# Moving the split of the output weights to the end of VectorE's step, and holding GpSimd's running sums 2 to 7 until the last low part of the step is written

## The chip, the cores and the metric

The kernel runs on one core of a Trainium2 chip. The metric is the device time of one execution in microseconds (us). The engines are TensorE (PE in the profile, with its weight loads as PEld), VectorE (DVE), ScalarE (ACT), GpSimd (POOL) and SyncE (SP), which starts the transfers.

## What is computed

Causal attention with 16 heads over two sequences of 1024 tokens, a layernorm, a mixture-of-experts block, and a second layernorm. The part that the change touches is the attention:

```python
q = rmsnorm(q, q_norm_w);  k = rmsnorm(k, k_norm_w)
q = apply_rope(q, ...);    k = apply_rope(k, ...)
scores = jnp.einsum('bhtd,bhsd->bhts', q, k) * scale
scores = LOGIT_SOFTCAP * jnp.tanh(scores / LOGIT_SOFTCAP)
scores = jnp.where(mask, -jnp.inf, scores)
attn = jax.nn.softmax(scores, axis=-1)
out = jnp.einsum('bhts,bhsd->bhtd', attn, v)      # B=2, H=16, T=1024, d=128
return out @ wo.T
```

## The kernel before

**Precision.** Every large product is made of three: each operand is kept as a high part (a rounded copy, suffix `_hi`) and a low part (what the rounding left, `_lo`), and TensorE adds hi·hi, hi·lo and lo·hi (`mm3`, lines 417 to 419). For most operands ScalarE writes the high part and VectorE the low one (`lo_of`, line 1098: source minus high part). For weights VectorE writes both (`split`, lines 1108 and 1098).

**Steps.** Attention is 32 steps, one per head and sequence. Heads go in pairs: the four steps of a pair have `q` = 0 to 3, where `k = q % 2` is the head of the pair and `q // 2` the sequence. I call them q0, q1, q2 and q3; there are 8 pairs. Step `s` computes the eight score tiles of its head and sequence (tile `j` is 128 keys by the `T - 128 j` queries from them on: 1024, 896, 768, 640, 512, 384, 256 and 128 columns). Within the same step TensorE also projects the queries and keys of step `s + 1` and finishes step `s - 1`: its last value products, the sums of its probabilities and its output projection. The code calls the work on step `s - 1` `old` and that on step `s + 1` `new`; the last step of all has no `new`.

**One tile's way.** TensorE `scores` to PSUM; ScalarE tanh and exp into `praw` in SBUF; GpSimd `mask` on the diagonal 128 columns (line 959); ScalarE the high part `prob_hi`; VectorE the low part `prob_lo` (`tile`, line 1202; signals `plo_done`); TensorE `values`. Besides, GpSimd adds the eight tiles of a step up in `pacc` (`accumulate`, lines 972 and 976: a copy for tile 0, then seven additions, from 896 down to 128 columns, which I call running sums 1 to 7). Each addition waits for the one ahead of it. When all eight are in, TensorE's `sums` multiplies `pacc` with ones (line 451), and VectorE turns that into `rsum`, by which it scales the output projection.

**Queues.** Each engine runs its own instructions in the order in which the code lists them, step after step; nothing but semaphores couples the engines. In a step TensorE's order is: projections `q0`, `q1` of the next step, old `values` 3, `scores` 0 (which waits for `qlo_done`, the low part of the step's queries), in odd steps a projection of values `vc`, `k0`, old `values` 4, `k1`, `scores` 1, old `values` 5 to 7, `ss` (sums of squares), `scores` 2 and 3, old `sums`, then the output projections `op0` to `op3` among further scores and values. Projections take turns in two PSUM banks: each waits until the second one ahead of it has been read (`pj_free`). The first two, `q0` and `q1`, are read by VectorE's copies to `qraw` (line 1165).

VectorE's order is in `step` below. Its last three pieces are the low part of the values `vb` or `vd`, the scaling of the next step's queries `scale_raw` (line 1183), and their split `split_queries` (`qhat_hi`, `qhat_lo`). The scaling needs a row of factors that GpSimd computes (`rq`, line 943, behind masks 0 and 1), VectorE transposes (line 1179), and SyncE sends through DRAM to all partitions (`rqB`).

The split of the output weights `wo` of one head (`split_output_weights`, two instructions on 128 by 256) runs in q0 and q1. Its product is read by TensorE at `op0` of the step after.

Of the kernel before, what the change touches and what calls it, by code (L numbers as in the profile page):

```python
# [27 lines left out]
TT = T // P  # L28
# [21 lines left out]
RING = TT  # L50
# [85 lines left out]
def block_kernel(nc, x, xT_d, wqkv_d, wo_d, qn, kn, cos_d, sin_d, gw_d, wgu_d, wd_d, wsgu_d, wsd_d, out):  # L136
# [5 lines left out]
    with ctx:  # L142
# [3 lines left out]
        def sem(name):  # L146
            return ctx.enter_context(nc.semaphore(name))
# [132 lines left out]
        mask_done, phi_done, plo_done = sem("mask_done"), sem("phi_done"), sem("plo_done")  # L280
# [646 lines left out]
        def _(pool):  # L927
# [12 lines left out]
            def rms_queries(b, count):  # L940

                pool.wait_ge(pj_free, count)
                nc.gpsimd.tensor_tensor(rq[:, 0:TT], var[:, b, 0:TT], mhalf[:, 0:TT], ALU.pow).then_inc(rq_done, 1)

            def rms_keys(b):
                nc.gpsimd.tensor_tensor(rk[:, b, :], var[:, b, TT:2 * TT], mhalf[:, TT:2 * TT], ALU.pow).then_inc(rk_done, 1)
# [6 lines left out]
            def mask(s, b, j):  # L953

                t = s * TT + j
                pool.wait_ge(exp_done, t + 1)
                diag = praw[:, raw_at(b, j)][:, 0:P]
                pool.sem_inc(waited, 1)
                nc.gpsimd.affine_select(out=diag, in_=diag, compare_op=ALU.is_ge, fill=0.0, base=0,  # L959
                                        pattern=[[1, P]], channel_multiplier=-1).then_inc(mask_done, 1)  # L960

            def accumulate(s, b, j):

                t = s * TT + j
                if j == 0 and not (isinstance(s, int) and s == 0):
                    pool.wait_ge(rsum_done, s)
                pool.wait_ge(mask_done, t + 1)
                raw = praw[:, raw_at(b, j)]
                if j == 0:

                    pool.sem_inc(waited, 1)
                    nc.gpsimd.tensor_copy(pacc[:, 0:P], raw[:, 0:P]).then_inc(pacc_done, 1)
                else:
                    before = praw[:, raw_at(b, 0)][:, P:T] if j == 1 else pacc[:, P * j:T]
                    pool.wait_ge(pacc_done, t + RING)
                    nc.gpsimd.tensor_tensor(pacc[:, P * j:T], before, raw, ALU.add).then_inc(pacc_done, 1)  # L976

            def next_head_weights(p, s):
                pool.wait_ge(qf_done, s + 1)
                pool.sem_inc(waited, 1)  # L980
                nc.gpsimd.tensor_copy(gcur[:, :], ghead[:, bass.ds(p * 2 + 2, 2)]).then_inc(gcur_done, 1)

            def step(st):

                s, k, old, new = st.s, st.k, st.old, st.new
                if old:
                    mask(s - 1, 1 - k, 6)
                    mask(s - 1, 1 - k, 7)
                    for j in range(TT):
                        accumulate(s - 1, 1 - k, j)  # L990
                if new and st.q == 3:
                    next_head_weights(st.pair, s)
                mask(s, k, 0)
                mask(s, k, 1)
                if new:
                    rms_queries(1 - k, st.unit("ss")[0])
                mask(s, k, 2)
                mask(s, k, 3)
                if new:
                    rms_keys(1 - k)  # L1000
                mask(s, k, 4)
                mask(s, k, 5)

            pool.wait_ge(zeros_out, 16 * ((2 * ACCR // P * D + T - 1) // T + 1))
            for q in range(STEPS):
                step(Step(0, q, "first"))
# [3 lines left out]
            for q in range(STEPS):  # L1010
                step(Step(NP_ - 1, q, "last"))
# [78 lines left out]
        def _(dve):  # L1090
# [5 lines left out]
            def lo_of(dst, x_, hi, done):  # L1096

                v.tensor_tensor(dst, x_, hi.bitcast(F32), ALU.subtract).then_inc(done, 1)  # L1098
# [7 lines left out]
            def split(pair_, at_, src, hi_sem, n, lo_sem):  # L1106

                v.tensor_copy(pair_[0][at_], src).then_inc(hi_sem, 1)
                dve.wait_ge(hi_sem, n)
                lo_of(pair_[1][at_], src, pair_[0][at_], lo_sem)  # L1110

            def split_next_weights(p, e, count):

                dve.wait_ge(w_in[e], p * 16 + 16)
                if count is not None:
                    dve.wait_ge(pj_done, count)
                split(wqk, (ALL, e), wraw[:, e], whi_done, p * 2 + e + 1, wlo_done)
# [52 lines left out]
            def values_in(what, group, count, bank_no):  # L1170
                dve.wait_ge(pj_done, count)
                dve.wait_ge(vhi_done, group + 1)
                two = slice(2 * V_TILES[what], 2 * V_TILES[what] + 2)
                lo_of(vS[1][:, two].rearrange("p j e d -> p (j e d)"), ps[:, bank_no, :],
                      vS[0][:, two].rearrange("p j e d -> p (j e d)"), pj_free)

            def turn_rms(step):
                dve.wait_ge(rq_done, step + 1)
                v.transpose(rqT[:, :], rq[:, :]).then_inc(rqT_done, 1)
# [19 lines left out]
            def tile(s, b, j):  # L1199
                dve.wait_ge(phi_done, s * TT + j + 1)  # L1200
                n = T - P * j
                lo_of(prob[1][:, AT[j]:AT[j] + n], praw[:, raw_at(b, j)], prob[0][:, AT[j]:AT[j] + n], plo_done)
# [11 lines left out]
            def output_lo(s):  # L1214
                dve.wait_ge(ohi_done, s + 1)
                lo_of(oT[1][:, :], ps[:, 4:6, :].rearrange("p k n -> p (k n)"), oT[0][:, :], o_evac)
# [8 lines left out]
            def split_output_weights(st):  # L1225

                e = st.q
                dve.wait_ge(wo_in[e], st.pair * 16 + 16)
                if not st.first:
                    dve.wait_ge(pj_done, st.unit("q0")[0] - 1)  # L1230
                split(wo, (ALL, e), woraw[:, e], wohi_done, st.pair * 2 + e + 1, wolo_done)

            def step(st):

                s, k, old, new = st.s, st.k, st.old, st.new
                if st.q < 2:
                    split_output_weights(st)
                if new:
                    projected("q0", 1 - k, s + 1, *st.unit("q0"))
                    projected("q1", 1 - k, s + 1, *st.unit("q1"))  # L1240
                if old:
                    tile(s - 1, 1 - k, 4)
                    tile(s - 1, 1 - k, 5)
                if k:
                    values_in("vc", st.group("vc"), *st.unit("vc"))
                if old:
                    tile(s - 1, 1 - k, 6)
                    tile(s - 1, 1 - k, 7)
                if new:
                    projected("k0", 1 - k, s + 1, *st.unit("k0"))  # L1250
                    projected("k1", 1 - k, s + 1, *st.unit("k1"))
                if old:
                    output_lo(s - 1)
                if new:
                    projected("ss", 1 - k, s + 1, *st.unit("ss"))
                    if st.b and not st.last:
                        split_next_weights(st.pair + 1, k, st.unit("q0")[0] - 1)
                if old:
                    summed(1 - k, *st.unit("sums"))
                    out_projected(st.old_b, 1 - k, 0, s - 1, *st.unit("op0"))  # L1260
                if new:
                    turn_rms(s + 1)
                tile(s, k, 0)
                if old:
                    out_projected(st.old_b, 1 - k, 1, s - 1, *st.unit("op1"))
                tile(s, k, 1)
                if not k:
                    values_in("va", st.group("va"), *st.unit("va"))
                elif st.q == 3 and new:
                    split_values_weights(st.pair + 1, st.unit("vc")[0])  # L1270
                if old:
                    out_projected(st.old_b, 1 - k, 2, s - 1, *st.unit("op2"))
                tile(s, k, 2)
                if old:
                    out_projected(st.old_b, 1 - k, 3, s - 1, *st.unit("op3"))
                tile(s, k, 3)
                if not k:
                    values_in("vb", st.group("vb"), *st.unit("vb"))
                elif new:
                    values_in("vd", st.group("vd"), *st.unit("vd"))  # L1280
                if new:
                    if st.q == 3:
                        dve.wait_ge(gcur_done, st.pair + 2)
                    scale_raw(s + 1, 1 - k)
                    split_queries(s + 1, 1 - k)
# [35 lines left out]
            end, s = Step(NP_, 0, "tail"), B * H  # L1321
# [182 lines left out]
```

## Time and profile before

| | |
|---|---|
| Time, median of 3 runs | 1117.14 us (1113.54 to 1119.96) |
| The profiled execution's own time | 1117.59 us |
| Its span in the trace | 1115.9 us |
| TensorE busy | 1023.3 us (92%) |
| VectorE busy | 840.0 us (75%) |
| ScalarE busy | 697.5 us (63%) |
| GpSimd busy | 642.0 us (58%) |
| Granted clock of TensorE, mean | 0.964 |

Busy times are sums over instructions. The profile's times count from the start of the span, so a step can be followed at its place: the fifth pair's steps q0, q1, q2 and q3 begin near 471.7, 498.7, 526.2 and 552.0 us (I take the end of `qhat_lo` on VectorE as the border of a step). A pair takes 108.15 us and the pairs repeat to a few hundredths.

### The profile page before, as it was taken

The numbers are of one execution on the slowest core, as the hardware profiler recorded it, in microseconds if no ns is written. First come the engines' busy times: TensorE is split into PE (matmuls) and PEld (weight loads), VectorE is DVE, ScalarE is ACT, GpSimd is POOL, SyncE is SP. The second block draws the span as 40 slices with busy tenths as digits, with TensorE's granted clock in tenths as the row PEclk, the third lists the DMA queues.
The fourth block names the chain that finished last, engine by engine and source line by source line (L and its number), as shares of the span: only waits on it lengthen the run. The fifth ranks groups of instructions, "written<-read, shape, count | busy, mean of one in ns | idle before, by whom it ended". The sixth has DMA issues, their size and how long they took to land.

```text
span 1115.9 us, 17459 instructions
## 1 busy us (share of the span) xinstructions
PE 1023.3 (92%) x6048; PEld 809.9 (73%) x6048; DVE 840.0 (75%) x1376; ACT 697.5 (63%) x1159; POOL 642.0 (58%) x660
## 2 busy tenths in 40 slices
PE   4699999999999999999999999999999859889865
PEld 3478878887888788888878887888788746345432
DVE  3389898989898989888998889888988775613103
ACT  3377767777777777777777777777777723222212
POOL 0167666666676666666666666666667542353232
PEclk8899999999999999999999999999999978989888
DMA  9111011101100100010001000100000019539327
GB/s 337 46 39 33 24 36 40 33 30 39 30 20 29 39 30 20 30 39 29 20 29 39 30 20 29 40 29 20 20 20 20 20 30 289 129 101 253 74 29 231
DMA packets 47256, 66.77 MB, mean 60 GB/s; under 512 B 7904, under 2 KB 38592, under 8 KB 47168
## 3 DMA queue, kind: packets, MB, share of 16 engines
q1 hardware_dynamic: 43376, 60.65, 17.7%
q0 software_dynamic: 3072, 4.46, 2.3%
q8 instruction: 48, 0.79, 0.3%
q10 hardware_dynamic: 720, 0.54, 0.1%
q14 instruction: 40, 0.33, 0.1%
HBM read 54.35 MB, written 11.29 MB: 59 GB/s over the span
## 4 chain that ended last, share of the span: by engine, by line
PE 64%; DVE 14%; DMA 9%; issue 6%; POOL 3%; ACT 3%; SPq 1%; DVEq 0%; POOLq 0%; ACTq 0%
PE ps L417 19%; PE ps L418 18%; PE ps L419 17%; DMA acc_rows<-ye,acci 7%; DVE prob_lo L1098 7%; PE ps L451 5%; DVE qraw L1165 2%; PE ps L594 2%; POOL pacc L976 2%; PE ps L638 1%; DMA yacc<-in_x 1%; DVE qhat_lo L1098 1%; DVE qraw L1183 1%; DVE kT_lo L1098 1%; PE ps L604 1%
## 5 line engine op out<-in xcount | busy, mean ns | idle before, releaser
L1098 DVE TENSOR_TENSOR prob_lo<-praw,prob_hi 128x1024 fp32r<-128x1024 f32 (+7 forms) x256 | 304.6, 1213 | 1.7 <-ACT prob_hi L753 1.7
L959 POOL TENSOR_SCALAR_AFFINE_SELECT praw<-praw 128x128 f32<-128x128 f32 x256 | 120.7, 472 | 275.1 <-ACT praw L805 255.8
L976 POOL TENSOR_TENSOR pacc<-pacc,praw 128x768 f32<-128x768 f32 (+2 forms) x192 | 233.1, 1214 | 27.7
L799 ACT ACTIVATE praw<-ps,rk 128x1024 f32<-128x1024 f32 (+7 forms) x256 | 185.8, 740 | 64.3 <-PE ps L419 60.3
L753 ACT ACTIVATE prob_hi<-praw 128x1024 fp32r<-128x1024 f32 (+7 forms) x256 | 168.6, 685 | 1.3 <-POOL praw L959 1.3
L805 ACT ACTIVATE praw<-praw 128x1024 f32<-128x1024 f32 (+7 forms) x256 | 167.9, 683 | 0.0
L417 PE MATMUL ps<-qhat_hi,kT_hi 128*128 128x512 f32 (+3 forms) x384 | 135.1, 352 | 10.5 <-DVE qhat_lo L1098 10.1
L417 PE MATMUL ps<-prob_hi,vS_hi 128*128 128x512 f32 (+3 forms) x384 | 136.0, 354 | 6.0 <-DVE prob_lo L1098 6.0
L418 PE MATMUL ps<-prob_lo,vS_hi 128*128 128x512 f32 (+3 forms) x384 | 133.3, 347 | 0.0
L418 PE MATMUL ps<-qhat_lo,kT_hi 128*128 128x512 f32 (+3 forms) x384 | 133.0, 346 | 0.0
L419 PE MATMUL ps<-qhat_hi,kT_lo 128*128 128x512 f32 (+3 forms) x384 | 132.8, 346 | 0.0
L419 PE MATMUL ps<-prob_hi,vS_lo 128*128 128x512 f32 (+3 forms) x384 | 132.5, 345 | 0.0
L417 PE MATMUL ps<-xT_hi,wqk_hi 128*128 128x512 f32 x256 | 103.3, 404 | 23.8 <-DVE xT_lo L1098 11.9
L1210 DVE SCALAR_TENSOR_TENSOR yacc<-ps,rsum,yacc 128x256 f32<-128x256 f32 x256 | 111.5, 477 | 6.7 <-PE ps L419 5.8
L418 PE MATMUL ps<-xT_lo,wqk_hi 128*128 128x512 f32 x256 | 102.2, 399 | 0.0
L419 PE MATMUL ps<-xT_hi,wqk_lo 128*128 128x512 f32 x256 | 101.8, 397 | 0.0
L417 PEld LDWEIGHTS ps<-qhat_hi,kT_hi 128*128 128x128 f32 x384 | 72.8, 190 | 30.8 <-issue 12.8
L417 PEld LDWEIGHTS ps<-prob_hi,vS_hi 128*128 128x128 f32 x384 | 72.6, 189 | 17.6 <-DVE prob_lo L1098 12.1
L774 ACT ACTIVATE ksq<-ps 128x512 f32<-128x512 f32 x64 | 38.3, 599 | 65.8 <-PE ps L419 65.8
L419 PEld LDWEIGHTS ps<-qhat_hi,kT_lo 128*128 128x128 f32 x384 | 72.7, 189 | 8.4
L419 PEld LDWEIGHTS ps<-prob_hi,vS_lo 128*128 128x128 f32 x384 | 72.4, 189 | 8.2
L418 PEld LDWEIGHTS ps<-qhat_lo,kT_hi 128*128 128x128 f32 x384 | 73.0, 190 | 6.0
(161 smaller groups left out, 2255.6 us busy)
## 6 DMA issues: line engine op xcount, KB each, us to landing
qsq<-rq_rows SPq DMA_DIRECT2D x32, 512.0 KB, 4.0
wgu<-in_wgu SPq DMA_DIRECT2D x16, 704.0 KB
wd<-in_wd SPq DMA_DIRECT2D x16, 352.0 KB
wraw<-in_wqkv SPq DMA_DIRECT2D x16, 256.0 KB, 4.5
acc_rows<-pacc SPq DMA_DIRECT2D x8, 512.0 KB, 10.5
wvraw<-in_wqkv SPq DMA_DIRECT2D x16, 128.0 KB, 2.7
woraw<-in_wo SPq DMA_DIRECT2D x16, 128.0 KB, 4.1
yacc<-in_x SPq DMA_DIRECT2D x1, 2048.0 KB, 13.8
```

The lines of the kernel that those rows point to most:

```text
L417: mm(out_, left[0], right[0], start=start, stop=False)
L418: mm(out_, left[0], right[1], start=False, stop=False)
L419: return mm(out_, left[1], right[0], start=False, stop=stop)
L451: last = mm(ps[32 * g:32 * g + 32, bank_no, c0:c0 + 32 * TT].rearrange("p (j r) -> p j r", r=32), ones[:, :], by_strip[:, g], start=True, ...
L753: return nc.scalar.activation(dst, src, ACT.Copy)
L774: nc.scalar.activation(ksq[:, cols], bank, ACT.Square).then_inc(ksq_done, 1)
L799: nc.scalar.activation(praw[:, raw_at(b, j)], buf[:, P * j:T], ACT.Tanh, scale=rk[:, b, j:j + 1]).then_inc(tanh_done, 1)
L805: nc.scalar.activation(tile, tile, ACT.Exp, scale=CAP).then_inc(exp_done, 1)
L959: nc.gpsimd.affine_select(out=diag, in_=diag, compare_op=ALU.is_ge, fill=0.0, base=0, pattern=[[1, P]], channel_multiplier=-1).then_inc(ma ...
L976: nc.gpsimd.tensor_tensor(pacc[:, P * j:T], before, raw, ALU.add).then_inc(pacc_done, 1)
L1098: v.tensor_tensor(dst, x_, hi.bitcast(F32), ALU.subtract).then_inc(done, 1)
L1210: last = v.scalar_tensor_tensor(y, ps[:, bank_no, D * i:D * i + D], rsum[:, k, 2 * u + i:2 * u + i + 1], y, ALU.mult, ALU.add)
```

## The change

Two edits. On VectorE the split of the output weights in q0 and q1 moves from the head of the step's list to its end, ahead of the scaling of the next step's queries. On GpSimd the additions 2 to 7 of the old step wait until VectorE has written the low part of the old tile 7.

```diff
@@ GpSimd, step @@
                 if old:
                     mask(s - 1, 1 - k, 6)
                     mask(s - 1, 1 - k, 7)
-                    for j in range(TT):
+                    for j in range(2):
+                        accumulate(s - 1, 1 - k, j)
+                    pool.wait_ge(plo_done, s * TT + RING)
+                    for j in range(2, TT):
                         accumulate(s - 1, 1 - k, j)
@@ VectorE, step @@
                 s, k, old, new = st.s, st.k, st.old, st.new
-                if st.q < 2:
-                    split_output_weights(st)
                 if new:
                     projected("q0", 1 - k, s + 1, *st.unit("q0"))
                     projected("q1", 1 - k, s + 1, *st.unit("q1"))
@@ VectorE, end of step @@
                     values_in("vb", st.group("vb"), *st.unit("vb"))
                 elif new:
                     values_in("vd", st.group("vd"), *st.unit("vd"))
+                if st.q < 2:
+                    split_output_weights(st)
                 if new:
```

The additions behind the last step (after the loop over steps) are as they were.

VectorE at the border from q3 to q0 of a pair. Before, the split stands between the queries' low part and the copies that free the two projection banks:

```order
L1183 SCALAR_TENSOR_TENSOR qraw<-qraw,gcur,qsq 128x1024 [waits rqB_in,gcur_done]
L1108 CAST qhat_hi<-qraw 128x1024 [waits qf_done]
L1098 TENSOR_TENSOR qhat_lo<-qraw,qhat_hi 128x1024 [waits qhi_done]
L1108 CAST wo_hi<-woraw 128x256 [waits pj_done,wo_in0]
L1098 TENSOR_TENSOR wo_lo<-woraw,wo_hi 128x256 [waits wohi_done]
L1165 COPY qraw<-ps 128x512 [waits qsq_done,qlo_done,pj_done]
L1165 COPY qraw<-ps 128x512 [waits qsq_done,pj_done]
L1098 TENSOR_TENSOR prob_lo<-praw,prob_hi 128x512 [waits phi_done]
```

In the changed kernel (lines are 3 further on) the copies follow the queries at once:

```order
L1186 SCALAR_TENSOR_TENSOR qraw<-qraw,gcur,qsq 128x1024 [waits rqB_in,gcur_done]
L1111 CAST qhat_hi<-qraw 128x1024 [waits qf_done]
L1101 TENSOR_TENSOR qhat_lo<-qraw,qhat_hi 128x1024 [waits qhi_done]
L1168 COPY qraw<-ps 128x512 [waits qsq_done,qlo_done,pj_done]
L1168 COPY qraw<-ps 128x512 [waits qsq_done,pj_done]
L1101 TENSOR_TENSOR prob_lo<-praw,prob_hi 128x512 [waits phi_done]
```

At this border the split has gone. It stands now at the next one, from q0 to q1 (and likewise from q1 to q2), ahead of the scaling:

```order
L1101 TENSOR_TENSOR prob_lo<-praw,prob_hi 128x640 [waits phi_done]
L1101 TENSOR_TENSOR vS_lo<-ps,vS_hi 128x512 [waits vhi_done,pj_done]
L1111 CAST wo_hi<-woraw 128x256 [waits pj_done,wo_in0]
L1101 TENSOR_TENSOR wo_lo<-woraw,wo_hi 128x256 [waits wohi_done]
L1186 SCALAR_TENSOR_TENSOR qraw<-qraw,gcur,qsq 128x1024 [waits rqB_in]
L1111 CAST qhat_hi<-qraw 128x1024 [waits qf_done]
L1101 TENSOR_TENSOR qhat_lo<-qraw,qhat_hi 128x1024 [waits qhi_done]
```

So the queries of steps q1 and q2 are ready later by the two instructions of a split, and those of q3 and q0 are not.

GpSimd's row in the changed kernel, one step's part (before, the same rows without `plo_done`):

```order
L972 COPY pacc<-praw 128x128 [waits rsum_done,mask_done]
L976 TENSOR_TENSOR pacc<-praw 128x896 [waits pacc_done,mask_done]
L976 TENSOR_TENSOR pacc<-pacc,praw 128x768 [waits pacc_done,mask_done,plo_done]
L976 TENSOR_TENSOR pacc<-pacc,praw 128x640 [waits pacc_done,mask_done]
L976 TENSOR_TENSOR pacc<-pacc,praw 128x512 [waits pacc_done,mask_done]
L976 TENSOR_TENSOR pacc<-pacc,praw 128x384 [waits pacc_done,mask_done]
L976 TENSOR_TENSOR pacc<-pacc,praw 128x256 [waits pacc_done,mask_done]
L976 TENSOR_TENSOR pacc<-pacc,praw 128x128 [waits pacc_done,mask_done]
L959 AFFINE_SELECT praw<-praw 128x128 [waits exp_done] x2
L943 TENSOR_TENSOR rq<-var,mhalf 128x8 [waits pj_free]
```

No row has moved; the third has one more wait, and all that stand behind it, masks 0 and 1 and `rq` too, are behind that wait.

## Rows read from the trace of the kernel before

**Rows 1.** Windows: busy time of each engine, granted clock, DMA share, from 130 to 800 us.

```profile
130.00:800.00 670.00, 658.17 (x4160) 553.82 (x4153) 592.46 (x835) 497.89 (x819) 443.16 (x452) 1.00 0.09 30
```

**Rows 2.** Waits of PE, 100 to 845 us: total, times, longest.

```profile
PE ps L417 <- DVE qraw L1165: 7.8, 7, 1.1
PE ps L417 <- DVE prob_lo L1098: 3.0, 7, 0.7
```

**Rows 3.** The same over the whole span.

```profile
PE ps L417 <- DVE qraw L1165: 12.9, 9, 3.8
```

**Rows 4.** Timeline, step q0 of the fifth pair: DVE, POOL, PE (idle before in brackets).

```profile
472.05 2.38 DVE L1098 TENSOR_TENSOR wo_lo<-woraw,wo_hi 128x256 fp32r<-128x256 f32 x1
472.02 2.12 POOL L976 TENSOR_TENSOR pacc<-praw 128x896 f32<-128x896 f32 x1 [0.16 <-POOL pacc L972]
475.08 0.50 PE L417 MATMUL ps<-xT_hi,wqk_hi 128*128 128x512 f32 x1 [1.12 <-DVE qraw L1165]
484.89 0.42 PE L451 MATMUL ps<-pacc,ones 128*32 128x256 f32 x4
```

**Rows 5.** Instructions on the tile wo_lo: ns min/median/max.

```profile
L1098 DVE TENSOR_TENSOR wo_lo<-woraw,wo_hi x16: 425/1396/2377, 41.5 to 823.4; 128x256 fp32r<-128x256 f32 x16
```

**Rows 6.** Groups of DVE by form: count, busy us, mean ns, idle before.

```profile
L1098 DVE TENSOR_TENSOR prob_lo<-praw,prob_hi 128x384 fp32r<-128x384 f32 x32 | 64.9, 2029 | 0.0
...
L1098 DVE TENSOR_TENSOR prob_lo<-praw,prob_hi 128x768 fp32r<-128x768 f32 x32 | 30.3, 948 | 0.5 <-ACT prob_hi L753 0.5
L1098 DVE TENSOR_TENSOR prob_lo<-praw,prob_hi 128x640 fp32r<-128x640 f32 x32 | 26.2, 819 | 0.7 <-ACT prob_hi L753 0.7
```

**Rows 7.** Timeline behind the last step: POOL and PE.

```profile
901.42 7.49 POOL L976 TENSOR_TENSOR pacc<-pacc,praw 128x768 f32<-128x768 f32 x6
...
909.06 0.65 PE L451 MATMUL ps<-pacc,ones 128*32 128x256 f32 x4 [7.02 <-POOL pacc L976]
```

**Rows 8.** Timeline, step q1 of the fifth pair: POOL, DVE, PE.

```profile
501.56 8.06 POOL L976 TENSOR_TENSOR pacc<-pacc,praw 128x768 f32<-128x768 f32 x6
...
504.33 0.69 DVE L1098 TENSOR_TENSOR vS_lo<-ps,vS_hi 128x512 fp32r<-128x512 f32 x1 [0.23 <-ACT vS_hi L753]
...
500.63 0.39 PE L417 MATMUL ps<-qhat_hi,kT_hi 128*128 128x512 f32 x1
...
512.62 0.64 PE L451 MATMUL ps<-pacc,ones 128*32 128x256 f32 x8
```

**Rows 9.** Timeline, step q2 of the fifth pair: DVE, POOL, PE.

```profile
524.21 0.69 DVE L1108 CAST qhat_hi<-qraw 128x1024 fp32r<-128x1024 f32 x1
524.93 1.23 DVE L1098 TENSOR_TENSOR qhat_lo<-qraw,qhat_hi 128x1024 fp32r<-128x1024 f32 x1
...
523.54 1.51 POOL L959 TENSOR_SCALAR_AFFINE_SELECT praw<-praw 128x128 f32<-128x128 f32 x2 [2.86 <-ACT praw L805]
...
526.46 2.12 POOL L976 TENSOR_TENSOR pacc<-praw 128x896 f32<-128x896 f32 x1 [0.15 <-POOL pacc L972]
...
526.88 0.39 PE L417 MATMUL ps<-qhat_hi,kT_hi 128*128 128x512 f32 x1
...
534.31 0.33 PE L417 MATMUL ps<-prob_hi,vS_hi 128*128 128x128 f32 x1 [0.39 <-DVE prob_lo L1098]
...
538.19 0.64 PE L451 MATMUL ps<-pacc,ones 128*32 128x256 f32 x8
...
537.93 0.52 DVE L1108 CAST wqk_hi<-wraw 128x512 fp32r<-128x512 f32 x1
```

**Rows 10.** Timeline, step q3 of the fifth pair: DVE, PE.

```profile
557.62 0.69 DVE L1098 TENSOR_TENSOR vS_lo<-ps,vS_hi 128x512 fp32r<-128x512 f32 x1 [0.32 <-ACT vS_hi L753]
...
565.91 0.64 PE L451 MATMUL ps<-pacc,ones 128*32 128x256 f32 x8
```

**Rows 11.** Timeline, the last step (q3 of the eighth pair): DVE, PE.

```profile
880.28 0.69 DVE L1098 TENSOR_TENSOR vS_lo<-ps,vS_hi 128x512 fp32r<-128x512 f32 x1 [2.63 <-ACT vS_hi L753]
...
887.54 0.42 PE L451 MATMUL ps<-pacc,ones 128*32 128x256 f32 x4 [1.33 <-POOL pacc L976]
```

## The prediction, written before the changed kernel ran

> **What bounds the kernel now.** I read the windows first. In the stretch of steady attention TensorE is busy 658.17 of 670 us at the full granted clock (2.4 GHz), VectorE 592, GpSimd 443 [rows 1]. So only what shortens or lengthens TensorE's own waits moves the end there, and all its idle time in the stretch is 12 us. Then the waits of TensorE: between 100 and 845 us it waits 7 times, 7.8 us in all, for VectorE's copy that frees a projection bank, and 7 times, 3.0 us, for a low part of a probability tile [rows 2]. Over the whole span the first of these has 9 waits and 12.9 us [rows 3]; less the 7 and one of 3.8 in the prologue, one of 12.9 - 7.8 - 3.8 = 1.3 us is left, in the first pair's q1.
>
> The timeline shows where the copy is late. At the head of q0 `wo_lo` starts at 472.05 and takes 2.38 us; GpSimd's addition of 896 columns has started at 472.02 and ends at 474.14. Only then does the split go on, the copies follow, and TensorE waits 1.12 us [rows 4]. Alone `wo_lo` takes 0.43 us, its minimum [rows 5]. The two engines exclude each other here: a low part of 384 columns takes 2.03 us in the mean where the one of 640 columns, which meets no addition, takes 0.82 [rows 6]. In q2 a value product waits 0.39 us for tile 7 [rows 9] in the same way.
>
> **The split moved.** In q0 the 1.12 us go: seven times, and 1.3 us once in the first pair. What it costs at its new place: the cast and `wo_lo`, about 0.3 + 0.43 = 0.72 us, delay the scaling and `qhat_lo`. In q1 the scores start at 500.63 [rows 8] where the queries' low part had been ready since the step's border at 498.7: 1.9 us, hidden. In q2 `qhat_lo` ends at 524.93 + 1.23 = 526.16 and the scores start at 526.88 [rows 9]: the new end is 526.88, so TensorE waits about 0.1 us. The factors' transfer has landed before the split, so it only gains slack. The load of the next pair's output weights, queued on SyncE behind the split of q1, starts some 6 us later and is needed two to three steps on; nothing waits for it.
>
> **The additions held.** VectorE wins most here: tiles 4 to 7 wait for one addition each. With the time of a low part falling by 0.13 us for each 128 columns (948 to 819 ns, [rows 6]), tiles 5 to 7 alone would take 0.55, 0.42 and 0.29 us. But TensorE waits for none of this except the 0.39 us in q2 and some in the last step. What it costs is on GpSimd: additions 2 to 7 start when tile 7 is done, and TensorE's `sums` waits for addition 7. From the first of the six to the end of the last takes 8.06 us now, in company [rows 8], and 7.49 us behind the last step, where no low part from SBUF interferes [rows 7]. I take 7.6: the small additions in mid-step meet nothing now and are still a few hundredths longer than at the end. From the end of the last addition to TensorE's start pass 909.06 - (901.42 + 7.49) = 0.15 us [rows 7]; I take as much for GpSimd's start behind VectorE.
>
> Step by step, against TensorE's present places:
> - q0: the 896 addition ends at 474.14 as now, tiles 4 to 7 follow in about 1.6 us (0.69 + 0.55 + 0.42 + 0.29, less the overlap of neighbours) to 475.7. Additions 475.9 to 483.5, product possible at 483.65. `sums` stands at 484.89 [rows 4], less the 1.12 us won: 483.77. No new wait. Net -1.12.
> - q1: tiles 6 and 7 stand behind the values `vc`, whose low part ends at 504.33 + 0.69 = 505.02 [rows 8], set by TensorE and ScalarE. Tile 7 ends at 505.57, additions 505.73 to 513.33, product at 513.48; `sums` stands at 512.62 [rows 8]. Net +0.86.
> - q2: the copy and the 896 addition wait now for `qhat_lo`, 0.72 us later. (GpSimd's masks end 0.15 us behind VectorE's cast: 523.54 + 1.51 = 525.05 against 524.21 + 0.69 = 524.90 [rows 9].) The addition runs 526.88 to 529.0, tiles to 530.6, additions 530.75 to 538.35; `sums` at 538.5 against 538.19 - 0.39 + 0.10 = 537.90 [rows 9]. The cast of `wqk_hi` on VectorE, 0.52 us at 537.93 [rows 9], now meets the last additions; I add 0.1. Net -0.39 + 0.10 + 0.7 = +0.4.
> - q3: `vc` ends at 558.31, tile 7 at 558.86, additions 559.02 to 566.62, product at 566.77 against 565.91 [rows 10]; 0.2 for the cast that meets them. Net +1.05.
> - last step: no `new` work, so `sums` comes early and waits for GpSimd already (1.33 us). Tile 7 at 880.28 + 0.69 + 0.55 = 881.53, additions to 889.3, product at 889.44 against 887.54 [rows 11]. Net +1.9.
>
> What stands behind the additions on GpSimd, masks 0 and 1 and `rq`, is late too, by about what `sums` is late; VectorE and ScalarE reach their waits for it as much later, since TensorE is. I cost it at nothing; if that cover fails, VectorE's transpose of `rq` adds tenths of a microsecond a step.
>
> Sum: a middle pair -1.12 + 0.86 + 0.4 + 1.05 = +1.2, six times = +7.2. First pair: q0 nothing old, q1 -1.3, its `sums` (held less there, since the 1.3 us came ahead of everything) put at no wait, q2 and q3 +1.45: +0.15. Last pair: -1.12 + 0.86 + 0.25 (no weights to cast) + 1.9 = +1.9. Together +9.2 us. On the profiled execution's 1117.59 that gives 1126.8; against the median of the runs, 1117.14 (0.45 lower), 1126.3.
>
> The Trainium skill, SBUF — State Buffer, section "Who interferes with whom", says that a VectorE instruction with at most one SBUF input, outside the two-port modes, does not contend with GpSimd. By that rule the kT and oT low parts, which read one input from PSUM, leave the six additions alone, and they take the 7.49 us of the tail: the sum would then be about +6.5 us instead of +9.2.
>
> **Rivals.**
> (a) Slower, as forecast: the sums wait. 0.76.
> (b) Faster: GpSimd's additions have enough slack, and only the removed waits count: 7 x 1.12 + 1.3 + 7 x 0.39 = 11.9 us less, 1105 us. For it: `sums` never waits for GpSimd in the steady stretch now [rows 2], and 501.56 + 8.06 + 0.15 = 509.77 is 2.85 us ahead of the product [rows 8]. Against it: in q1 and q3 the hold is 4.2 us (505.73 for 501.56), more than that. It decides where the six additions take 512.62 - 0.15 - 505.73 = 6.7 us; the shortest seen is 7.49. 0.07.
> (c) The two cancel. With 7.49 us for the six and nothing for the casts a middle pair comes to -1.12 + 0.75 + 0.2 + 0.75 = +0.6, the last pair +1.2, the first -0.4, together +4.4: 1121.5. 0.14 with all that ends within 0.5%.
> (d) Much slower: the additions keep today's 8.06 us, since VectorE's later work from SBUF meets them; 0.46 more in three steps of every pair and some 0.3 in q0: 9.2 + 24 x 0.46 + 7 x 0.3 = 22 us, 1139. Less than 0.05, a part of (a)'s chance.
> (e) The scaling of the queries begins to wait for its factors (GpSimd's `rq`, transpose, transfer), which it never does now in the steady stretch. The split ahead of it adds 0.72 us of room in q0 and q1; in q3 `rq` is 1.05 us late as TensorE is. If half a microsecond a step came of it, 1126.3 + 16 x 0.5 = 1134. 0.03.
>
> **How the numbers follow.** A measurement of this kernel tells about 0.5% (5.6 us) from no change. Forecast 1126.3. Range: down to (c)'s lower part, 1119, and up to 1133 (additions between 7.6 and 8.06 everywhere). Faster by over 0.5%: (b), 0.07. Within 0.5%: (c), 0.15. Slower: (a), (d), (e), 0.78.
>
> **What would show it.** `wo_lo` at 0.43 us in all 16, low parts 5 to 7 at 0.55, 0.42 and 0.29 us, VectorE's busy time some 100 us lower (the tiles of 384 columns alone give 31 x (2.03 - 0.55) = 46, `wo_lo` 8 x 1.95 = 16). No wait of TensorE for the copies to `qraw`. New waits of TensorE on `pacc` in q1, q2, q3: three a pair, 0.7 to 1.0 us each, and over 3 us in the last step. Pairs of 108.15 + 1.2 = 109.3 us. I am wrong if the six additions take less than 7.4 us together, if `sums` finds addition 7 done in q1 and q3, or if pairs get shorter.

## The result

The changed kernel takes 1123.38 us in the median of 7 runs (1121.13 to 1127.64), against 1117.14 us (7 runs too, 1113.54 to 1119.96) before: a ratio of 1.0068, 95% interval 1.0045 to 1.009. It is slower, by 6.2 us in the medians; 9.2 were forecast. The profiled execution has a span of 1120.8 us.

The head of the page after. VectorE is 107 us less busy than before, GpSimd 27, and the kernel is slower:

```profile
span 1120.8 us, 17459 instructions
PE 1019.0 (91%) x6048; PEld 810.8 (72%) x6048; DVE 733.0 (65%) x1376; ACT 699.7 (62%) x1159; POOL 615.5 (55%) x660
```

TensorE's waits after, over the whole span. The wait for the copies to `qraw` is down from nine to one, in the prologue (before: [rows 3]). In its place stands a wait for the additions in `pacc`, once in each of the 31 steps that have an old one, and once behind the last:

```profile
PE ps L451 <- POOL pacc L976: 32.3, 32, 7.0
PE ps L417 <- DVE qraw L1168: 2.3, 1, 2.3
```

Between 100 and 850 us (before: [rows 2]) it is the one large wait. The second row, 0.17 us a time, is a gap at the projection `vd` of q3 that was 0.11 us before:

```profile
PE ps L451 <- POOL pacc L976: 19.4, 28, 0.8
PE ps L417 <- DVE yacc L1213: 1.2, 7, 0.2
```

The fifth pair after, step by step: GpSimd's additions 2 to 7 and the product that needs them (in brackets the idle time before, and its releaser). They answer to [rows 4] and [rows 8 to 10]:

```profile
475.83 7.64 POOL L976 TENSOR_TENSOR pacc<-pacc,praw 128x768 f32<-128x768 f32 x6 [1.63 <-DVE prob_lo L1101]
483.62 0.42 PE L451 MATMUL ps<-pacc,ones 128*32 128x256 f32 x4 [0.53 <-POOL pacc L976]
504.35 7.64 POOL L976 TENSOR_TENSOR pacc<-pacc,praw 128x768 f32<-128x768 f32 x6 [3.83 <-DVE prob_lo L1101]
512.13 0.42 PE L451 MATMUL ps<-pacc,ones 128*32 128x256 f32 x4 [0.73 <-POOL pacc L976]
530.04 7.72 POOL L976 TENSOR_TENSOR pacc<-pacc,praw 128x768 f32<-128x768 f32 x6 [1.64 <-DVE prob_lo L1101]
537.91 0.42 PE L451 MATMUL ps<-pacc,ones 128*32 128x256 f32 x4 [0.69 <-POOL pacc L976]
558.65 7.72 POOL L976 TENSOR_TENSOR pacc<-pacc,praw 128x768 f32<-128x768 f32 x6 [4.29 <-DVE prob_lo L1101]
566.51 0.42 PE L451 MATMUL ps<-pacc,ones 128*32 128x256 f32 x4 [0.81 <-POOL pacc L976]
```

Read them in twos. Each product starts 0.14 to 0.15 us behind the end of the six additions (504.35 + 7.64 = 511.99, product at 512.13). GpSimd had been idle ahead of them, for 1.6 us in even steps and about 4 us in odd ones, where tiles 6 and 7 stand behind the values `vc`. The six are faster than the 8.06 us before, but by 0.4 us only.

**What a wait costs.** The profile's idle time in front of an instruction is not what the wait costs. TensorE's program is the same in both kernels, so matmul number n can be compared with itself. At the head of q0 before, and after:

```profile
473.57 0.39 PE L419 MATMUL ps<-qhat_hi,kT_lo 128*128 128x512 f32 x1
475.08 0.50 PE L417 MATMUL ps<-xT_hi,wqk_hi 128*128 128x512 f32 x1 [1.12 <-DVE qraw L1165]
475.42 0.40 PE L418 MATMUL ps<-xT_lo,wqk_hi 128*128 128x512 f32 x1
```

```profile
473.62 0.39 PE L419 MATMUL ps<-qhat_hi,kT_lo 128*128 128x512 f32 x1
473.85 0.39 PE L417 MATMUL ps<-xT_hi,wqk_hi 128*128 128x512 f32 x1
474.07 0.39 PE L418 MATMUL ps<-xT_lo,wqk_hi 128*128 128x512 f32 x1
```

From start to start 1.51 us before and 0.23 after: the wait cost 1.28, not 1.12. The idle time is counted from the modelled end of the matmul ahead, 0.39 us behind its start, where the next one would have started 0.23 us behind it; the 0.16 between them are lost as well. The next matmul costs 0.11 more (0.34 for 0.23). That is 1.39 us for the wait.

Four more gaps of 0.10 to 0.12 us go in the same step: two at the product with the old tile 4, one at that with the old tile 7, one at the sums of squares just behind it. No view lists a wait there, but they aren't the copies' doing. In the run with the hold alone, told below, the copies' wait is as before and all four gaps are gone. The product with tile 4 before, and in that run:

```profile
476.36 0.39 PE L419 MATMUL ps<-xT_hi,wqk_lo 128*128 128x512 f32 x1
476.71 0.50 PE L417 MATMUL ps<-prob_hi,vS_hi 128*128 128x512 f32 x1
477.05 0.40 PE L418 MATMUL ps<-prob_lo,vS_hi 128*128 128x512 f32 x1
```

```profile
482.08 0.39 PE L419 MATMUL ps<-xT_hi,wqk_lo 128*128 128x512 f32 x1
482.31 0.39 PE L417 MATMUL ps<-prob_hi,vS_hi 128*128 128x512 f32 x1
482.54 0.39 PE L418 MATMUL ps<-prob_lo,vS_hi 128*128 128x512 f32 x1
```

Before, tile 4's low part ends at 476.66, 0.05 us ahead of the product; with the hold it ends 0.35 us ahead (481.96). So late low parts cost TensorE 0.46 us in q0 without a wait in any list. With the copies' 1.39 that makes 1.85 us won in the step.

TensorE's 6048 matmuls can all be compared in this way. The fifth pair's changes, in start times, beside the prediction's terms:

| Step | What changes | Measured, us | Forecast, us |
|---|---|---|---|
| q0 | copies' wait, with the matmul behind it | -1.39 | -1.12 |
| q0 | four small gaps at tiles 4 and 7 | -0.46 | 0 |
| q0 | `sums` waits | +0.60 | 0 |
| q1 | `sums` waits | +0.80 | +0.86 |
| q2 | scores wait for `qhat_lo` | +0.18 | +0.10 |
| q2 | tile 7 in time | -0.77 | -0.39 |
| q2 | `sums` waits | +0.76 | +0.7 |
| q3 | `sums` waits, and 0.06 at `vd` | +0.94 | +1.05 |
| pair | | +0.66 | +1.2 |
| last step | | +3.3 | +1.9 |

The same first projection of q0 follows one pair later at 583.21 before (108.13 us on) and at 582.65 after (108.80 us on).

The two spans differ by 4.9 us. The changed kernel is 1.7 us ahead at the first scores of attention; from there the first pair loses 0.16, the six middle pairs 3.5 together (7.2 forecast), the last pair 2.9 (1.9 forecast). Five middle pairs lose 0.66; the third loses 0.27, since before the change its wait for tile 7 in q2 was 0.66 us and not 0.39.

The last step after. TensorE reaches `sums` early and waits 4.53 us there; what it runs then is slower: a matmul of 512 columns takes 0.63 us for 0.40, and the next starts 0.43 us later instead of 0.23:

```profile
890.85 0.91 PE L451 MATMUL ps<-pacc,ones 128*32 128x256 f32 x8 [4.53 <-POOL pacc L976]
893.57 0.63 PE L418 MATMUL ps<-qhat_lo,kT_hi 128*128 128x512 f32 x1
894.00 0.63 PE L419 MATMUL ps<-qhat_hi,kT_lo 128*128 128x512 f32 x1
```

The windows of this kernel say why. Behind the busy times of the five engines stands the granted clock: 0.76 in the mean of the six microseconds around the end of the wait, 1.00 ahead of it. For the three microseconds from 891 to 894 it is 0.51, so nearly all of them were granted 1.2 instead of 2.4 GHz:

```profile
883.00:888.00 5.00, 3.33 (x22) 2.70 (x20) 1.29 (x2) 4.79 (x6) 4.57 (x3) 1.00 0.00 0
888.00:894.00 6.00, 3.15 (x17) 2.30 (x18) 1.20 (x4) 3.52 (x5) 2.99 (x7) 0.76 0.00 1
891.00:894.00 3.00, 3.00 (x17) 2.12 (x12) 1.20 (x4) 3.00 (x4) 0.42 (x2) 0.51 0.01 3
894.00:900.00 6.00, 6.00 (x38) 5.49 (x37) 6.00 (x11) 3.69 (x7) 2.69 (x4) 0.96 0.00 0
```

Of the step's 3.3 us the later start of `sums` is 1.76 and the slow stretch behind it 1.56.

### The profile page after: what moved, and what is told of

Read it like the earlier page. It is cut to its first block, busy times and chain, and to the rows that moved or that the text cites. A ratio compares the mean times of both kernels' runs of the same rounds, so it can differ in the third digit from the quotient of the medians.

```text
span 1120.8 us, 17459 instructions
## 1 busy us (share of the span) xinstructions
PE 1019.0 (91%) x6048; PEld 810.8 (72%) x6048; DVE 733.0 (65%) x1376; ACT 699.7 (62%) x1159; POOL 615.5 (55%) x660
## 4 chain that ended last, share of the span: by engine, by line
PE 40%; POOL 23%; DVE 18%; DMA 8%; issue 7%; ACT 3%; SPq 0%; POOLq 0%; DVEq 0%; ACTq 0%
POOL pacc L976 20%; PE ps L417 11%; PE ps L418 11%; PE ps L419 11%; DVE prob_lo L1101 6%; DMA acc_rows<-ye,acci 6%; DVE qraw L1186 2%; DVE qhat_lo L1101 2%; DVE yacc L1213 2%; PE ps L594 2%; PE ps L451 2%; ACT vS_hi L753 1%; PE ps L638 1%; DVE qraw L1168 1%; DVE vS_lo L1101 1%
## 5 line engine op out<-in xcount | busy, mean ns | idle before, releaser
L976 POOL TENSOR_TENSOR pacc<-pacc,praw 128x768 f32<-128x768 f32 (+2 forms) x192 | 222.5, 1159 | 109.6 <-DVE prob_lo L1101 86.5
L959 POOL TENSOR_SCALAR_AFFINE_SELECT praw<-praw 128x128 f32<-128x128 f32 x256 | 114.7, 456 | 226.3 <-ACT praw L805 206.3
L1101 DVE TENSOR_TENSOR prob_lo<-praw,prob_hi 128x1024 fp32r<-128x1024 f32 (+7 forms) x256 | 203.0, 817 | 2.3 <-ACT prob_hi L753 2.2
L417 PE MATMUL ps<-prob_hi,vS_hi 128*128 128x512 f32 (+3 forms) x384 | 133.6, 348 | 1.7 <-DVE prob_lo L1101 1.7
L417 PE MATMUL ps<-xT_hi,wqk_hi 128*128 128x512 f32 x256 | 102.1, 399 | 14.2 <-DVE xT_lo L1101 11.9
L1101 DVE TENSOR_TENSOR kT_lo<-ps,kT_hi 128x512 fp32r<-128x512 f32 x64 | 44.3, 692 | 72.8 <-ACT kT_hi L753 72.8
L976 POOL TENSOR_TENSOR pacc<-praw 128x896 f32<-128x896 f32 x32 | 75.7, 2366 | 4.9 <-POOL pacc L972 4.9
```

What stands on the lines that cost most here:

```text
L417: mm(out_, left[0], right[0], start=start, stop=False)
```

## The experiments

Theory A is the prediction's, corrected: only TensorE's own waits count, each edit has its own, and they add up by start times. Theory B: the two edits work through the exclusion between VectorE and GpSimd, so whatever frees VectorE is good. "Pair" is the mean distance of the same matmul from one middle pair to the next in the profiled execution (108.22 us before, the longer third pair included, 108.79 in the changed kernel). All timed kernels ran beside the kernel before on the same chip.

| Kernel | Median, us | Before there, us | Ratio (95%) | Pair, us |
|---|---|---|---|---|
| split moved only | 1110.21 | 1115.08 | 0.9959 (0.9937 to 0.998) | 107.31 |
| hold only | 1133.8 | 1115.08 | 1.0164 (1.0135 to 1.0194) | 110.15 |
| changed, hold in even steps only | 1104.18 | 1115.08 | 0.9902 (0.9869 to 0.9935) | 107.04 |
| changed, no hold in the last step | 1117.36 | 1115.08 | 1.0021 (0.9999 to 1.0042) | 108.78 |
| only q0's split moved | 1122.3 | 1116.81 | 1.0049 (1.0029 to 1.007) | 108.58 |
| the same, hold 2 to 7 in even steps | 1119.01 | 1116.81 | 1.0021 (1.0002 to 1.0041) | 108.31 |
| the same, hold 4 to 7 in even steps | 1109.14 | 1116.81 | 0.9938 (0.9921 to 0.9956) | 107.17 |
| both splits moved, hold 4 to 7 in even steps | 1095.6 | 1116.81 | 0.9815 (0.979 to 0.9841) | 105.86 |
| both splits moved, hold 4 to 7 in all steps | 1096.13 | 1116.51 | 0.9814 (0.9796 to 0.9832) | 105.82 |
| both splits moved, hold 6 and 7 in all steps | 1105.78 | 1116.51 | 0.9908 (0.9895 to 0.9922) | 107.33 |

**Split moved, nothing held.** The changed kernel with the hold taken out:

```diff
-                    for j in range(2):
-                        accumulate(s - 1, 1 - k, j)
-                    pool.wait_ge(plo_done, s * TT + RING)
-                    for j in range(2, TT):
+                    for j in range(TT):
                         accumulate(s - 1, 1 - k, j)
```

> The split moved, the additions not held. Theory A (what counts is TensorE's own waits, and each edit has its own): the copies' wait in q0 goes, which by start times of the same matmul was 1.87 us with what follows it, not 1.12; 0.18 us come at the head of q2; and since low parts and additions exclude each other as before, tile 7 is again late for TensorE in q0 and q2, by about 0.5 us. No wait on pacc in the steady pairs. A pair about 1 us shorter than before, 1109 us. Theory B (the gain of the changed kernel comes from the fewer exclusions between VectorE and GpSimd, and the place of the split matters little): no change, 1117.

It is faster than before, by 0.4%, and a pair is 0.9 us shorter (1.0 was expected). No wait on `pacc` in the steady pairs; TensorE's waits between 100 and 845 us are those for tile 7 in q0 and q2, the first of them new:

```profile
PE ps L417 <- DVE prob_lo L1098: 5.7, 13, 0.5
```

Theory B gave no change; the pair's 0.9 us speak against it, and the next run, where it gave 1117 to 1123 us, more plainly.

**Hold only.** The kernel before with GpSimd's edit alone.

> The additions held, the split where it was. Theory A: the copies' wait in q0 stays, and TensorE waits for addition 7 in every step: about 0.5 us in q0, 0.8 in q1, 0.75 in q2 against 0.77 won at tile 7, 0.9 in q3, 3.5 in the last step: a pair 2.2 us longer, about 1136 us. Theory B: VectorE is some 90 us less busy, so the kernel is not slower than the changed one: 1117 to 1123.

It is 1.6% slower, with the pair 1.9 us longer (2.2 expected): 0.73 us more at `sums` in q0 against 0.46 won at the four small gaps, 0.80 in q1, 0.75 in q2 against 0.77 won at tile 7, and 0.94 in q3 with its gap at `vd`. Theory B falls. Between 100 and 845 us TensorE now has both waits:

```profile
PE ps L451 <- POOL pacc L976: 19.5, 27, 0.9
PE ps L417 <- DVE qraw L1168: 7.8, 7, 1.1
```

The two edits' effects on a pair, -0.91 and +1.93 us, add up to +1.02; together they give +0.57, since in q0 and q2 they work on the same low parts: with the split alone TensorE gets tile 4 in time in q0 and waits 0.40 us for tile 7 instead, and the hold has both in time. So the slowdown is the hold's, and the split pays a part of it back.

**Hold in even steps only.** `if j == 2 and not k: pool.wait_ge(plo_done, s * TT + RING)` in the loop.

> The changed kernel with the hold in q0 and q2 only. Theory A: the waits on pacc in q1 (0.80), q3 (0.88) and the last step (3.2 and what follows) go, those in q0 and q2 stay: a pair about 1.1 us shorter than before, 1108 us. If instead the hold is paid back in the odd steps as well (by tile 7 coming early), it stays near the changed kernel's 1123.

As theory A says: 1.0% faster, the pair 1.2 us shorter. Of TensorE's waits on `pacc` in the steady pairs half are left, two a pair (100 to 835 us):

```profile
PE ps L451 <- POOL pacc L976: 8.7, 14, 0.7
```

In odd steps the hold from addition 2 on is nothing but loss: TensorE never waited for tile 7 there, and tile 7 comes late anyway, behind `vc`.

**No hold in the last step.** `if j == 2 and st.new:`.

> The changed kernel without the hold in the last step alone. Theory A: only that step's loss goes, 3.5 us by the start times (3.2 of wait, the rest matmuls at half rate behind it), 1.1 us of it were won back at tile 7: about 3.0 us less than the changed kernel, 1120. If the half rate has another cause, 2.2 us less.

Its first matmul behind the wait starts 1.7 us earlier than in the changed kernel, and the third score product 3.0 us earlier. The granted clock stays at 1.00, and the product of 512 columns is back at 0.40 us:

```profile
888.00:894.00 6.00, 4.81 (x36) 4.17 (x37) 3.85 (x9) 6.00 (x9) 1.98 (x6) 1.00 0.01 1
```

```profile
889.19 0.64 PE L451 MATMUL ps<-pacc,ones 128*32 128x256 f32 x8 [1.33 <-POOL pacc L976]
890.81 0.40 PE L418 MATMUL ps<-qhat_lo,kT_hi 128*128 128x512 f32 x1
```

Against the kernel before it loses nothing in this step. So one hold more costs 3.3 us, almost half of it by the clock. The timed ratios, 1.0068 and 1.0021, lie 0.5% apart, more than 3.3 us, but come from two sets of runs, with the kernel before at 1117.14 and at 1115.08 us.

**Only q0's split moved.** q1's stays at the head of its step; nothing is held.

```diff
+                if st.q == 1:
+                    split_output_weights(st)
                 if new:
                     projected("q0", 1 - k, s + 1, *st.unit("q0"))
...
+                if st.q == 0:
+                    split_output_weights(st)
```

> Only q0's split moved (to the end of q0), q1's stays at the head of q1, nothing held. Theory A: against the run with both moved, the 0.18 us at the head of q2 and the growth of tile 7's wait there (0.10) go, 0.3 us a pair: a pair 1.1 us shorter than the kernel before, 0.6% to 0.7% faster. Theory C (the split costs nothing at q1's end, the 0.18 us there is paid in any case): the same as with both moved, 0.4% faster.

A miss: 0.5% slower than before, where theory A said 0.6 to 0.7% faster; the pair is 0.36 us longer. The timeline of q1 in this kernel, GpSimd and VectorE:

```profile
500.58 1.28 POOL L972 COPY pacc<-praw 128x128 f32<-128x128 f32 x1
502.01 2.12 POOL L976 TENSOR_TENSOR pacc<-praw 128x896 f32<-128x896 f32 x1 [0.15 <-POOL pacc L972]
```

```profile
500.44 1.26 DVE L1098 TENSOR_TENSOR qhat_lo<-qraw,qhat_hi 128x1024 fp32r<-128x1024 f32 x1
502.04 2.38 DVE L1098 TENSOR_TENSOR wo_lo<-woraw,wo_hi 128x256 fp32r<-128x256 f32 x1
504.34 1.28 DVE L1165 COPY qraw<-ps 128x512 f32<-128x512 f32 x2
```

q0's split delays the queries of q1 by 0.7 us; GpSimd's copy of tile 0, which now meets `qhat_lo`, ends 0.15 us behind it; and the addition of 896 columns starts 0.03 us ahead of `wo_lo`. The low part takes 2.38 us and the copies are late: TensorE waits 0.58 us for the first of them (0.86 by start times), and a projection behind it starts 0.6 us late as well. In the kernel before, the same two came in the other order in q1, where `wo_lo` takes its 0.43 us (its minimum in [rows 5]): the addition starts at 499.27, and the low part had started at 499.01. The cost has only moved from q0 to q1. The Trainium skill, SBUF — State Buffer, section "Who interferes with whom", puts it as "Issue order, not op shape, decides who blocks"; these rows agree, 0.43 us when `wo_lo` is 0.26 us ahead and 2.38 when it is 0.03 us behind.

**The same with additions 2 to 7 held in even steps.**

> Only q0's split moved; additions 2 to 7 held in q0 and q2. Theory A: as the run that holds in even steps with both splits moved, less 0.18 us at the head of q2 and some 0.4 of its wait on pacc, since the 896 addition there no longer waits for queries that are 0.72 us late: a pair 1.9 us shorter than before, about 1.3% faster. Theory C: the same as that run, 1.0% faster.

A miss for the same reason: the pair is 108.31 us where the one with both splits moved has 107.04. It tells nothing more than the run above.

**Both splits moved, additions 4 to 7 held in even steps.** `if j == 4 and not k:`.

> Both splits moved; in q0 and q2 only additions 4 to 7 held, nothing in odd steps. Theory A: GpSimd is idle about 0.4 us less in an even step than with additions 2 to 7 held, and tile 7 is still in time: the waits on pacc of 0.61 and 0.78 us fall by 0.4 each: a pair 0.8 us shorter than with the hold from 2, 1.4% faster than before. If the hold must keep every low part free (the exclusion theory), it loses what it won at tiles 5 and 6: 1.0% or less.

Better than expected, 1.85% faster than before. The profile lists no wait of TensorE at all between 100 and 835 us. In q0 of the fifth pair:

```profile
464.82 3.96 POOL L976 TENSOR_TENSOR pacc<-pacc,praw 128x768 f32<-128x768 f32 x2
469.34 3.96 POOL L976 TENSOR_TENSOR pacc<-pacc,praw 128x512 f32<-128x512 f32 x4 [0.56 <-DVE prob_lo L1100]
473.50 0.42 PE L451 MATMUL ps<-pacc,ones 128*32 128x256 f32 x4
```

GpSimd is idle 0.56 us instead of 1.63, the additions end at 473.30, and `sums` stands at 473.50 without a wait. Tiles 5 and 6 wait behind additions 2 and 3 as before the change, and nobody minds. VectorE is busy 573 of 650 us here (130 to 780), against 488 in the changed kernel, and the kernel is 28 us faster than that one in the medians:

```profile
130.00:780.00 650.00, 649.20 (x4127) 550.58 (x4126) 573.32 (x830) 494.10 (x814) 443.44 (x449) 1.00 0.10 31
```

**Only q0's split moved, additions 4 to 7 held in even steps.**

> Only q0's split moved; in q0 and q2 only additions 4 to 7 held, nothing in odd steps. Theory A: nearly all of TensorE's waits in a steady pair are gone, one of 0.2 us on pacc in q0 left: a pair 2.4 us shorter than before, about 1100 us, 1.6% faster, the fastest of all.

Expected the fastest, and 0.6% faster only: again q1's `wo_lo` behind the addition, 2.38 us. TensorE's waits in q1 that come of it, for the copies (4.1 us, 7 times) and a low part of values (2.3 us, 7 times), are all that the profile lists between 100 and 835 us.

**The hold from 4, and from 6, in all steps.** `if j == 4:` and `if j == 6:`.

> Both splits moved, additions 4 to 7 held in every step. Theory A: in odd steps additions 2 and 3 now fill the time in which VectorE waits for the values, so GpSimd is hardly idle there and sums finds addition 7 done; the even steps are those of the run with the hold from 4 in even steps: the same time as that, 1.8% faster than before, give or take 0.3%. If any hold across the values' projection is paid for in odd steps, 0.5 us in 15 steps, it is near 1.2% faster.

> Both splits moved, additions 6 and 7 held in every step. Theory A: tile 7 of the even steps waits behind addition 4, which is no longer held, so a hold from 6 changes nothing for it: TensorE's wait for tile 7 comes back (0.56 us in q0, 0.65 in q2), and the time is that of the run without any hold, 0.4% faster than before. If a hold from 6 does as well as one from 4, the wait for tile 7 had another cause.

The first is as fast as the one held in even steps (ratios 0.9814 and 0.9815, pairs 105.82 and 105.86 us). In q1 of the fifth pair GpSimd is idle 0.56 us ahead of addition 4 (3.83 ahead of addition 2 in the changed kernel): additions 2 and 3 fill the time in which VectorE waits for `vc`, and the hold in odd steps then costs nothing. The second has TensorE's waits for tile 7 back, as in the run without a hold:

```profile
PE ps L417 <- DVE prob_lo L1100: 5.8, 13, 0.5
```

Its pair takes 107.33 us (that run's 107.31), and in a whole pair no matmul's distance from the one ahead differs by over 0.05 us between the two. The timed ratios of these two equal kernels, 0.9908 and 0.9959, were taken on different chips and differ by more than their intervals; the trace decides, and half a per cent between runs on different chips should not be read. Each ratio in the table has the sign of its pair's change.

## Why the prediction came out as it did

The direction and the mechanism were right: held sums make TensorE wait for `pacc`. The time lies 2.9 us under the forecast, inside the range, but that nearness is in part luck: the middle pairs lost half of what was forecast (3.5 us for 7.2), the last pair a microsecond more than forecast (2.9 for 1.9). The steps, as the prediction put them:

- **"In q0 the 1.12 us go."** Right in kind, too small: 1.39 us. The error is reading the cost of a wait from the idle time in front of the instruction: the first projection starts 1.28 us earlier, the next matmul wins 0.11 more.
- **"But TensorE waits for none of this except the 0.39 us in q2 and some in the last step."** Wrong in q0: the late low parts of tiles 4 and 7 cost 0.46 us there, in gaps that no list of waits shows, and the run with the hold alone wins them back.
- **q0, "No new wait."** Wrong, and the other side of these two errors. The additions ended at 483.47 (forecast 483.5), but TensorE came at about 483.0 instead of 483.77, and waited. The net of q0, -1.25, was nearly that of the forecast, -1.12.
- **q1, "+0.86", and q3, "+1.05".** Measured +0.80 and +0.94. The row of six takes 7.64 and 7.72 us (7.6 taken); the cast of `wqk` costs under 0.1.
- **q2, "+0.4".** Measured +0.17. The scores do wait for the later queries (+0.18). Tile 7's wait was worth 0.77 by start times, not 0.39: the same misreading.
- **Last step, "+1.9".** Mis-sized: +3.3. `sums` itself came 1.76 us later, near the forecast; that TensorE's clock is granted at half behind the wait of 4.53 us, 1.56 us more, was not in the sum.
- **First pair, "+0.15".** Measured from the first scores of attention to the end of the pair: +0.16, by errors that cancel. `sums` in q1, "put at no wait", waited 0.73 us (+0.80); the scores of q1 waited for the later queries (+0.35); and the waits that went in q1 were worth 2.15 by start times, not 1.3.
- **"I cost it at nothing"**, of masks and `rq` behind the hold: right but for 0.06 us at `vd` in q3.
- VectorE's busy time, "some 100 us lower": 107. `wo_lo` takes 0.43 us in all 16, the low parts 5 to 7 take 0.55, 0.41 and 0.32 us in the mean (0.55, 0.42 and 0.29 forecast).
- **Rival (b)**, 0.07, faster by the removed waits alone, 11.9 us: by start times they are worth more, and where nothing is paid for them (both splits moved, additions 4 to 7 held) the kernel is 21 us faster than before. What failed in (b) is that `sums` has no slack for this hold. The decision point named for it, additions of 6.7 us, is far from the 7.64 seen. **Rival (c)** took 7.49 us and no cast, 1121.5: nearer to the measured time than the forecast, by the wrong step, since the additions were as slow as forecast and it was the waits removed that were worth more. (Its chance stands as 0.14 there and 0.15 in the sum.)
- The rule of the Trainium skill that a VectorE instruction with one input from SBUF, outside the two-port modes, leaves GpSimd alone (SBUF — State Buffer, "Who interferes with whom"): by it the six should take the tail's 7.49 us. They take 7.64 in q0 and q1, where VectorE runs hardly any others. The 0.15 us between are small, and I don't know their cause.

What stays open: the prologues of the two profiled executions differ, by 1.7 us at the first scores in favour of the changed kernel, in a place that the change doesn't touch. In the other ten kernels, alike up to there, the first scores lie between 1.4 us ahead of the kernel before and 0.1 behind it, so this looks like a difference between executions and not an effect of the change; what makes it is open. `sums` later in TensorE's order was not tried.

## What to carry to other kernels

In this kernel, where two engines exclude each other, holding one back helped only where the bound engine was late for the other's result; let the held one go on until the last collision that matters, here additions 2 and 3 before the hold, and the same edit turns from 0.7% slower to 1.9% faster. Count a wait by the distance between starts of the same instruction in the two traces, not by the idle time in front of it, and look for small gaps elsewhere that no list of waits shows; a run with one edit alone tells whose they are. Before moving an instruction, look which of the two excluding instructions starts first at its new place and at every later one: 0.3 us decided over 1.95 us here.

## What the runs showed of the hardware

A low part of 256 columns (`wo_lo`) takes 0.43 us alone and 2.38 us when GpSimd's addition of 896 columns started 0.03 us ahead of it. Behind a wait at a projection or at a product with a probability tile TensorE loses a further 0.10 to 0.12 us at the second matmul (0.34 us between starts instead of 0.23 at 512 columns); behind the waits at `sums` it does not. After one wait of 4.53 us its matmuls ran at about half rate (0.43 us between starts of 512 columns, granted clock 0.51 from 891 to 894 us); after the waits up to 1.33 us in the steps they did not.
